# Attention rounds: a group's scores and the values of two groups back put side by side on TensorE, two output projections issued later

## The reference, cut to what matters

```python
def reference(x, ctx, mask, g_xattn, g_ffn, Wq, Wk, Wv, Wo, ...):
    # attention: q from layernorm(x), k and v from ctx
    scores = einsum('bhqd,bhkd->bhqk', qh, kh) + attn_mask
    probs = softmax(scores, axis=-1)
    ctx = einsum('bhqk,bhkd->bhqd', probs, vh)
    x = x + tanh(g_xattn) * einsum('bse,de->bsd', ctx, Wo)
    # experts: one shared, 8 routed of which each token takes the best 2
    xf = layernorm(x)
    probs = sigmoid(xf @ router_w.T + routing_bias); top 2, weights divided by their sum
    x = x + tanh(g_ffn) * (shared(xf) + sum of the two weighted experts)
    return x
```

## Time and profile before

| | |
|---|---|
| time, median of 3 runs | 178.73 us (178.04 to 178.86) |
| profiled execution, first to last instruction (span) | 177.0 us |
| PE busy | 163.7 us (93%) |
| DVE busy | 127.1 us (72%) |
| ACT busy | 109.9 us (62%) |
| POOL busy | 110.7 us (63%) |
| the loop of three passes in the trace | from about 24.7 to 106.6 us |

### The profile page before, as it was taken

How to read it: one execution, slowest core, us unless ns; L and a number is a source line. 1 busy time by engine, 2 the same in 40 slices (tenths; PEclk the granted TensorE clock), 3 DMA queues, 4 the chain that set the end, 5 groups by cost and what they waited for, 6 DMA issues and landing times.

```text
span 177.0 us, 4529 instructions
## 1 busy us (share of the span) xinstructions
PE 163.7 (93%) x1412; PEld 139.0 (79%) x1412; DVE 127.1 (72%) x612; ACT 109.9 (62%) x404; POOL 110.7 (63%) x139
## 2 busy tenths in 40 slices
PE   7999889999999999999999999988899999998970
PEld 7777669997879998779998787986587878776860
DVE  2879988755898676888676979877857676665273
ACT  4567997558697447787646968744546666655300
POOL 3775799846786835868624768687644466656611
PEclk9999999999999999999999999999999999999996
DMA  5899995810000000000000000012222222220272
GB/s 151 280 373 378 414 403 206 352 62 0 19 2 4 15 2 4 30 21 15 30 4 0 15 21 15 17 50 54 85 76 66 74 63 67 63 77 31 57 233 90
DMA packets 11094, 17.33 MB, mean 98 GB/s; under 512 B 2075, under 2 KB 6945, under 8 KB 10944
## 3 DMA queue, kind: packets, MB, share of 16 engines
q1 hardware_dynamic: 9504, 14.59, 24.0%
q0 software_dynamic: 1280, 2.20, 3.8%
q10 hardware_dynamic: 288, 0.26, 0.4%
HBM read 9.99 MB, written 7.51 MB: 99 GB/s over the span
## 4 chain that ended last, share of the span: by engine, by line
PE 54%; DVE 12%; ACT 10%; POOL 9%; DMA 6%; issue 6%; SPq 1%; DVEq 0%; POOLq 0%
PE misc L408 8%; PE s_even L371 6%; PE o_bank L397 6%; ACT probs L722 4%; PE pt L382 4%; PE proj_q L328 4%; PE pt L658 3%; DMA ys<-probsT,xg 3%; PE proj_k L328 3%; DVE probs L931 3%; PE misc L482 3%; PE proj_q L329 2%; PE proj_q L330 2%; PE proj_k L330 2%; POOL ys L1436 2%
## 5 line engine op out<-in xcount | busy, mean ns | idle before, releaser
L722 ACT ACTIVATE probs<-probs,negmax 128x128 f32<-128x128 f32 x128 | 50.0, 394 | 8.5 <-DVE negmax L931 8.5
L1327 POOL TENSOR_TENSOR probs<-probs,rinv 128x512 f32<-128x512 f32 x32 | 33.1, 1048 | 24.4 <-DVE rinv L945 24.3
L1436 POOL DMA_INDIRECT ys<-probsT,xg x23 | 22.6, 982 | 17.1 <-issue 10.1
L722 ACT ACTIVATION_READ_ACCUMULATOR probs<-probs,negmax 128x1 f32 x128 | 24.3, 190 | 0.0
L931 DVE CUSTOM_DVE_ANT_0 probs<-s_even,mask 128x128 f32<-128x128 f32 x64 | 18.1, 283 | 3.8 <-issue 3.8
L1357 POOL DMA_INDIRECT xs<-xrow,slot x16 | 16.3, 1020 | 6.8 <-issue 3.9
L382 PE MATMUL pt<-ident_sb,probs 128*128 128x128 f32 x128 | 17.6, 277 | 1.6 <-POOL probs L1327 1.0
L371 PE MATMUL s_odd<-kT,qT 64*128 64x128 f32 x128 | 18.5, 285 | 0.0
L371 PE MATMUL s_even<-kT,qT 64*128 64x128 f32 x128 | 18.5, 284 | 0.0
L931 DVE CUSTOM_DVE_ANT_0 probs<-s_odd,mask 128x128 f32<-128x128 f32 x64 | 18.1, 283 | 0.0
L658 PEld LDWEIGHTS pt<-down_sb,v 128*128 128x128 f32 x92 | 12.1, 190 | 7.6 <-issue 7.5
(11 more groups left out here) (282 smaller groups left out, 458.8 us busy)
## 6 DMA issues: line engine op xcount, KB each, us to landing
xs<-pad SPq DMA_DIRECT2D x5, 858.0 KB, 6.3
xg<-xs SPq DMA_DIRECT2D x23, 66.0 KB, 1.9
down_sb<-down SPq DMA_DIRECT2D x1, 1152.0 KB, 9.6
probs<-ys SPq DMA_DIRECT2D x4, 256.0 KB, 4.0
gu_raw<-gu SPq DMA_DIRECT2D x3, 256.0 KB, 5.8
wk_raw<-wkT SPq DMA_DIRECT2D x2, 256.0 KB, 3.6
wq_raw<-wqT SPq DMA_DIRECT2D x2, 256.0 KB, 4.8
mask<-mask SPq DMA_DIRECT2D x8, 64.0 KB, 1.9
```

The costliest lines, as they stand in the source:

```text
L722: e = act.activation(probs[:, r, l, :], probs[:, r, l, :], ACT.Exp, bias=negmax[:, r, l:l + 1], scale=-1.0, accum_out=rowsum[:, r, l:l + 1])
L1327: pool.tensor_tensor(quad, quad, rinv[:, r, 4 * u:4 * u + 4].unsqueeze(2).to_broadcast([P, 4, P]), ALU.mult).then_inc(norm_done, 1)
L1436: pool.indirect_dma_start(out=ys, out_offset=bass.IndirectOffsetOnAxis(ap=xg[n % IN_FLIGHT][:, P:P + 1].bitcast(U32), axis=0), in_=y_sb[n ...
```

## The change

The same instructions are issued, in another order. On TensorE, `scores(g+n)` is moved down in each of the four rounds until it stands right ahead of `values` of two groups back. The projection that stood between them (or, in the second round, the output projection and a unit of q and k) is now ahead of the scores or behind the values. `out_project(2p)` stands behind `values(g+2)`, `out_project(2p+1)` behind `project_v(p+1, 1)`. ScalarE's and VectorE's programs follow: the copies of the projected units come ahead of the exps and of `mask_max`, and `x2_split` ahead of `copy_q`. The code ahead of the loop and behind it is the same.

```diff
@@ TensorE @@
                 transposes(g + 1, 1)
-                scores(g + 3, p, 3)
                 if p:
                     x2_transposes(p - 1)
...
                 project(p + 1, 0, "k")
+                scores(g + 3, p, 3)
                 values(g + 1, p, 1)
...
-                scores(g + 4, p + 1, 0)
-                out_project(2 * p, use, (ez_ready, p) if p else None)
                 project(p + 1, 2, "q")
                 project(p + 1, 2, "k")
+                scores(g + 4, p + 1, 0)
                 values(g + 2, p, 2)
+                out_project(2 * p, use, (ez_ready, p) if p else None)
...
+                project_v(p + 1, 0)
                 scores(g + 5, p + 1, 1)
-                project_v(p + 1, 0)
                 values(g + 3, p, 3)
 
                 transposes(g + 4, 0)
+                project_v(p + 1, 1)
                 out_project(2 * p + 1, use + 1, (at_ready, p) if p else None)
                 scores(g + 6, p + 1, 2)
-                project_v(p + 1, 1)
                 values(g + 4, p + 1, 0)
@@ ScalarE @@
                 copy_pt(g + 1, 1)
+                if p:
+                    x2_split(p - 1)
                 copy_q(p + 1, 0)
                 exps(g + 3, 3, 0)
-                if p:
-                    x2_split(p - 1)
...
                 exps(g + 4, 0, 0)
+                exps(g + 4, 0, 1)
                 copy_q(p + 1, 3)
-                exps(g + 4, 0, 1)
...
+                copy_v(p + 1, 0)
                 exps(g + 5, 1, 0)
-                copy_v(p + 1, 0)
...
+                copy_v(p + 1, 1)
                 exps(g + 6, 2, 0)
-                copy_v(p + 1, 1)
@@ VectorE @@
                 copy_pt(g + 1, 1)
-                mask_max(g + 3, p, 3, after(4, copy_k, p + 1, 0))
+                copy_k(p + 1, 0)
+                mask_max(g + 3, p, 3)
...
                 copy_pt(g + 2, 2)
+                copy_k(p + 1, 2)
                 mask_max(g + 4, p + 1, 0, choose_steps(p - 1) if p else iter(()))
-                copy_k(p + 1, 2)
...
+                copy_v(p + 1, 0)
                 steps = norm2_steps(2 * p, use)
...
                 run(steps, 1)
-                copy_v(p + 1, 0)
...
                 copy_pt(g + 4, 0)
+                copy_v(p + 1, 1)
                 add_attention(2 * p + 1, use + 1)
...
                 run(steps, 1)
-                copy_v(p + 1, 1)
```

## The result

The changed kernel took 180.75 us in the median of 4 executions (179.99 to 181.61), the kernel before on the same chip 178.78 (4 executions): ratio 1.0101 [1.0070, 1.0133]. With two more sets of the same kernel, on two other chips, there are 18 executions, median 180.44 (179.73 to 181.61), median span 178.35. So the change costs about 1.4 us, 0.8%. I had forecast 0.5 us, "within 0.5%" as the likeliest; the range to 180.8 held the first median by 0.05 us, which was luck. The profiled execution took 180.04, span 177.9, so it is one of the quicker ones.

A forecast was written before the change was run, and what follows sets the result against it. TensorE's program inside the loop was taken to bound the kernel. Shape changes -2.2, output projection -1.7 and router's transposes +4.45 gave +0.5 us, so 179.2 us of time; range 177.4 to 180.8.

The forecast's parts named there:

- What bounds the kernel: Inside the loop, TensorE's program sets the time; it holds 54% of the chain that ended last.
- The router's transposes: On TensorE they would wait 1.55 us for `xrow`, three times; cost 4.45 us with slower starts.
- The output projection of the fourth round: Behind the projection of v, its wait for `oT` goes; 1.7 us saved with the slower starts.
- Shape changes: TensorE's array changes shape three times a round instead of four; 0.19 in ten rounds, 0.15 in two, 2.2 us saved.
- The copies on ScalarE and VectorE: Copies of projected units, moved ahead of exps and `mask_max`, would stay hidden and cost nothing.
- The one that was forecast: The wait for `xrow` takes back the gain: +0.5 us; chance 0.53.
- the same: The outcome within 0.5% of the kernel before, 178.2 to 179.6 us; chance 0.53.
- The *faster* one: TensorE's delay is absorbed behind the loop or waits are under 1.1 us: 174.8 to 177.5 us; chance 0.20.
- the *slower* one: The delay also reaches the router's next step, in p = 1 and 2: 180.2 halfway, 182 us at most; chance 0.27.
- The change does nothing: TensorE's program is not the limit, so waits only move elsewhere; within "the same", no chance of its own.

The follow-up runs named there:

- the separator: Changed kernel plus a small full-array matmul between scores and values in each of twelve rounds: 184.17 us, ratio 1.0276 to the kernel before.
- the output projection's experiment: Changed kernel with the fourth round's output projection put back ahead of the projection of v: 184.12 us, ratio 1.0279 to the kernel before.
- fillers: Changed kernel plus six warm-up matmuls on TensorE in each of the three waits for `xrow`: 181.59 us, ratio 1.0149 to the kernel before.

## Why the forecast was right and wrong

**What bounds the kernel** held: waits put on TensorE or taken from it inside the loop appeared in the time (2.65 us less at the loop's end gave 2.5, 3.5 more gave 4.0).

**The router's transposes** held, mechanism and nearly size. Forecast was 4.45 us, of which 0.1 for slower starts; by the rows it is 2.01 + 1.56 + 1.57 - 0.40 = 4.74. The 0.40 is what the kernel before waited behind the loop, 106.60 - 105.36 - 0.84. The chain from the scores of g+6 was put at 4.60 and is 107.89 - 103.37 = 4.52; TensorE's side was put at 3.05 and is 2.95 (1.09 + 1.02 + 0.84). The two errors cancel in p = 1 and behind the loop, where 1.55 was forecast. In p = 0 the chain took 0.44 more, because of GpSimd; I had taken it from the p = 2 row alone.

**The output projection of the fourth round** held: no idle before L408. Its run from 101.49 to 103.37 takes 1.88, as one that does not wait, against the 1.98 of the earlier trace rows. With 0.84 for the transposes the waits that went are 0.45, 0.63 and 0.64, and with 0.1 each for the starts that makes 2.0 us where 1.7 was forecast.

**Shape changes** is the mis-sized term. Forecast -2.2, measured -1.5. It is what is left of the 1.29 at L434 behind the loop: 4.74 - 2.02 - 1.50, and 0.07 by which the loop's first transposes already start later. What was wrong is to charge 0.19 to each of ten rounds, of which 0.10 was to be the entry into the full array, read from a slow first matmul of the projection in the earlier trace rows. That slowness has nothing to do with the shape. The kernel before shows it behind the output projection, which is at the full array too:

```profile
62.08 0.36 PE L328 MATMUL proj_q<-xT_hi,wq_hi 128*128 128x256 f32 x1
62.28 0.28 PE L329 MATMUL proj_q<-xT_hi,wq_lo 128*128 128x256 f32 x1
```

And in the kernel after, where the projection of the second round now stands behind the logits:

```profile
59.67 0.37 PE L450 MATMUL misc<-router_sb,x_raw 128*128 128x8 f32 x2
59.90 0.36 PE L328 MATMUL proj_q<-xT_hi,wq_hi 128*128 128x256 f32 x1
60.10 0.28 PE L329 MATMUL proj_q<-xT_hi,wq_lo 128*128 128x256 f32 x1
```

Both are 0.20 where 0.11 is the pace. The first matmul of a projection takes it behind every kind of work that stands ahead of one in the two traces (0.20 to 0.23), so moving the projection doesn't save it. Round by round, from transposes to transposes, the gain is 0.07 to 0.11 in the second and third rounds of p = 1 and 2, 0.22 and 0.12 in p = 0, whose second round has no logits, 0.07 in the first round of p = 0, and 0.11 in each fourth round beyond the wait and its slower start. That is nearer to the 0.09 for leaving a shape than to 0.19. The first rounds of p = 1 and 2 gained 0.23 and 0.19, a little more than their 0.15. These last two and the 0.11 hang on the 0.84 for the transposes; the other rounds don't. Why the separator costs 0.20 where a change of shape saved gives about 0.1 is not shown by any run.

**The copies on ScalarE and VectorE** cost nothing: PE's waits name neither a bank of the projection nor a probability of g+5; the one wait of 0.3 for `normalise` is in both kernels. The exps' idle time rose from 8.5 to 19.9 us, and cost nothing.

**Sum.** Forecast +0.5, by the rows +1.3, and the median spans say +1.35. In the median time, with its share of executions near 181.5, +1.4. Of the 0.8 us missed, the shape changes are 0.7 and the router's transposes 0.3; the output projection gave 0.3 more than forecast. The 1.73 us by which the text ahead of the prediction and the prediction itself set a time above its span compares a median with another execution: within one execution the record has 1.75 to 2.21, 2.05 in the median. The forecast of 179.2 doesn't suffer, since it adds 0.5 to the median time.

**Rivals.** The one that was forecast names the mechanism, but its bound of "the same" was missed. The *faster* one was refuted by its own condition: the waits are over 1.1 us. (By the prediction's own terms, waits of 1.0 give -1.1 and not -1.2.) Of the *slower* one the mechanism did not happen (L449 and L408 do not wait), though its sign did. *The change does nothing* is refuted by the output projection's experiment, 4.0 us from one call moved.

## What to carry to other kernels

When work is taken out from between the start of a cross-engine chain and its consumer, the consumer loses its cover: count what is left on the consumer's engine, and move the consumer too. Here moving one call behind twelve matmuls turned a loss of 0.8% into a gain of 0.8%. And price a repeated small step at each place where it stands after the change: what seems to belong to the neighbour that goes may belong to the work itself, and come back behind the next one. Last, take the length of a run without a wait from a place that has none; one that is worked out by subtraction carries its error into every wait that is read with it.

## What the runs showed of the hardware

- VectorE's write of `xrow` (128 x 256, f32) took 0.38 to 0.46 us without GpSimd's split beside it. Beside the tensor_tensor of that split it took 0.41 to 1.53 us and ended 0.14 to 0.16 us behind the end of that instruction; another tensor_tensor of GpSimd (L1328), which starts while the write runs, did not lengthen it.
- A small full-array instruction between two half-array runs costs 0.20 us more than the same instruction behind full-array work. One change of shape less in a round, with no instruction taken away, saved 0.07 to 0.12 us in most rounds. The first 256-column matmul of a projection is followed by the next one 0.20 to 0.23 later instead of 0.11, also where the work ahead of it is at the full array.
- In one of five profiles with an idle time of about 1.75 us at the same place, the granted clock was 0.50 from 54 to 57 us and the pass took 1.55 us longer. An execution of the same kernel with a mean granted clock of 0.998 was slower still. Why 4 of 18 executions of the changed kernel, and 5 of 6 of it with fillers, are 1.3 us longer stays open.
